# The first feed-forward product of a retention network, taken in two f32r parts in every step of the later layers

## Chip, cores and metric

The kernel runs on one core of one Trainium2 chip. The metric is the device time of one execution in microseconds (us); the figure given for a kernel is the median over several runs.

## What is computed

The input x holds 8 sequences of 512 tokens with 128 features. It is normalized, and two branches start from the result: four layers of a retention network (here "attn"), and one layer of eight experts of which each token uses one (here "ffn"). The reference, cut to what matters:

```python
def block(h, p):                                  # one of four layers
    wk, w1, b1, w2, b2, gg, gb, wf1, bf1_, wf2, bf2_, lg, lb = p
    r = _retention(h, wk)
    m = r @ w1 + b1
    a, gate = jnp.split(m, 2, axis=-1)
    m = a * jax.nn.silu(gate) @ w2 + b2
    m = _groupnorm1(m, gg, gb)
    y = m + h
    f = jax.nn.gelu(y @ wf1 + bf1_, approximate=False) @ wf2 + bf2_
    return (_layernorm(f + y, lg, lb), None)

# experts: each token through the one with the greatest router logit
h = jax.nn.gelu(x_flat @ w1[e] + b1[e], approximate=False)
y = h @ w2[e] + b2[e]
# result
xn = _layernorm(x, axis=-1)
g = _silu(_L0_ffn_ref(xn, gate_w, w1, b1, w2, b2))
x = x + s * g                                     # s: the four layers' output
```

The change is about `y @ wf1`: 128 features into 256, for 512 tokens of one sequence at a time.

## The kernel before

Work goes in steps `(l, t)`: layer l from 0 to 3, t from 0 to 7, and three steps behind them. A step is a slot of a software pipeline over the 32 pairs of layer and sequence. Step t takes sequence t through the retention, sequence t-1 through the gate and the second product up to `y_sb`, sequence t-2 through the feed-forward part (`gelu_first`, `gelu_second`), and sequence t-3 through its LayerNorm and back into both layouts, `htok` (tokens on the partitions) and `hT` (features on the partitions). Every engine has its own hand-written order of the step's pieces, and the engines meet by semaphores. Each engine works through its own list in order.

The experts' work is cut in 39 tiles of 128 slots, worked off in the steps of layers 1 to 3. A step has two places for a tile, EARLY and LATE. `TURNS` (L263) gives the steps t = 0, 3 and 5 only the LATE place and the other five both:

```python
TURNS = [[LATE] if t in (0, 3, 5) else [EARLY, LATE] for t in range(B)]
```

A tile's first product ends in `bank5`, and ScalarE takes it through four Gelus of 128x128 into `h_T` (`tile_gelu`, L612, instructions of L618). For the LATE tile of step t this is done at the end of the same step when step t+1 has an EARLY tile (L714), and otherwise within step t+1, as `tile_gelu(late_turn_before(l, t))` (L677). So the steps t = 0, 3 and 5 are those with four Gelus of the tile before in their midst.

The first feed-forward product is `gelu_first` (L1234), called twice in a step, for the halves k = 0 and k = 1 of the 256 output features; half k is written to `bank[3 + k]`. Bank 3 also holds the gate's product of the same step, which ScalarE reads twice, as `th_sb` (L629) and `gg_sb` (L631); the second reading raises `gg_done`. Half 0 waits for `gg_done` (L1247), half 1 does not.

The product has two forms. In the plain form it is one f32 product of `all_f1` and `y_sb` (L1255, two matrix instructions). In the parted form ScalarE rounds `y_sb` to f32r, `y_h` (L673), VectorE makes the rest, `y_l` = `y_sb` - `y_h` (L963), and `parts_product` (L1228) makes three f32r products into the same bank: L1230, L1231 and L1232. The weights' parts `f1_parts` are made once by GpSimd. `parted(l, t)` chooses the form, and with it three more things: the order of the halves (`halves`: 0, 1 if parted, otherwise 1, 0), the place of `zhat_by_feature` on TensorE (the transposes of the normalized rows, L1264, ahead of the halves if parted, otherwise behind), and the place of the gate's two readings on ScalarE:

```python
if not parted(l, t):
    gate(l, t)
layernorm(l, t)
tile_gelu(late_turn_before(l, t))
if parted(l, t):
    gate(l, t)
```

Names used below: `q_sb` is ScalarE's copy of the query product, `zhat` the LayerNorm's output (its first two quarters by VectorE, L1074, its last two by ScalarE, L640), `A_sb` the masked scores (VectorE, L971), L978 and L988 VectorE's two operations that join gate and value into `gg_sb`, L1372 the second product, L1359 and L1361 the retention's output.

Of the kernel before, what the change touches and what calls it, by code (L numbers as in the profile page):

```python
# [17 lines left out]
def retention_moe_kernel(nc, x, Wkqv, Wm1, bm1, Wm2, bm2, gn_g, gn_b, Wf1, bf1, Wf2, bf2, ln_g, ln_b,  # L18
# [9 lines left out]
    B, S, D = x.shape  # L28
    L = Wkqv.shape[0]
# [20 lines left out]
    with ctx:  # L50
# [210 lines left out]
        EARLY, LATE = range(2)  # L261
        FIRST_TURNS = [(B - 1, EARLY), (B - 1, LATE)]
        TURNS = [[LATE] if t in (0, 3, 5) else [EARLY, LATE] for t in range(B)]  # L263
        assert sum(map(len, TURNS)) == TURN_TILES and EARLY not in TURNS[0]

        def turn(l, t, place):


            if isinstance(l, int) and (l == 0 or l >= L):
                if l == 0 and (t, place) in FIRST_TURNS:  # L270
                    j = FIRST_TURNS.index((t, place))
                    return j, TURN_TILES - TILE_LAG + j
                return None
            if place not in TURNS[t]:
                return None
            k = sum(map(len, TURNS[:t])) + TURNS[t].index(place)
            return (l - 1) * TURN_TILES + TILE_LAG + k, k
# [10 lines left out]
        def parted(l, t):  # L288


            return turn(l, t, EARLY) is not None and not (l == 0)

        def parted_steps(l, t):

            early = [k for k in range(B) if EARLY in TURNS[k]]
            return (l - 1) * len(early) + early.index(t) + 1

        def halves(l, t):

            return (0, 1) if parted(l, t) else (1, 0)  # L300
# [291 lines left out]
        def _(act):  # L592
# [72 lines left out]
            def step(l, t):  # L665
# [4 lines left out]
                if parted(l, t):  # L670
                    w = at(l, t, 2, B, LB)
                    act.wait_ge(y_done, w[0] + 1)
                    act.activation(y_h[:, :], y_sb[:, :], ACT.Copy).then_inc(y_high, 1)  # L673
                if not parted(l, t):
                    gate(l, t)
# [45 lines left out]
        def _(dve):  # L721
# [227 lines left out]
            def step(l, t):  # L949
# [11 lines left out]
                if parted(l, t):  # L961
                    dve.wait_ge(y_high, parted_steps(l, t))
                    dve.tensor_tensor(y_l[:, :], y_sb[:, :], y_h[:, :], ALU.subtract).then_inc(y_split, 1)  # L963
# [155 lines left out]
        def _(pe):  # L1119
# [114 lines left out]
            def gelu_first(l, t, i):  # L1234

                if w := at(l, t, 2, B, LB):
                    n, b, li = w
                    k = halves(l, t)[i]
                    if parted(l, t):
                        if t in (1, 2):  # L1240
                            pe.wait_ge(part_made, parts_made("f1", li))
                        pe.wait_ge(y_split, parted_steps(l, t))
                    else:
                        pe.wait_ge(y_done, n + 1)
                    need(pe, G_done, 2 * n)
                    if k == 0:
                        need(pe, gg_done, n + 2 if not (isinstance(n, int) and n + 2 > LB) else LB)  # L1247
                    else:
                        if not (l == 0):
                            need(pe, xtT_done, turns_before(l, t, LATE))  # L1250
                    cols = slice(k * D, (k + 1) * D)
                    if parted(l, t):
                        parts_product(bank[3 + k], f1_parts[:, li], cols, y_h, y_l, pe_f1)
                    else:
                        mm(bank[3 + k][:, :], all_f1[:, li, cols], y_sb[:, :], start=True, stop=True).then_inc(pe_f1, 1)  # L1255
# [167 lines left out]
```

## Time and profile before

| | us |
|---|---|
| median of 3 runs | 517.68 |
| lowest and highest | 517.53, 518.33 |
| profiled execution, device time | 517.43 |
| profiled execution, span in the trace | 515.4 |
| TensorE busy in the span | 469.9 (91%) |
| VectorE busy | 386.7 (75%) |
| ScalarE busy | 261.5 (51%) |
| GpSimd busy | 251.6 (49%) |

Engines are named PE (TensorE matrix instructions), PEld (its weight loads), DVE (VectorE), ACT (ScalarE), POOL (GpSimd) and SP (SyncE) in the profile. Times in a row are microseconds from the span's start. The 2.0 us between the span and the device time lie around the span.

### The profile page before, as it was taken

The numbers are of one execution on the slowest core, as the hardware profiler recorded it, in microseconds if no ns is written. First come the engines' busy times: TensorE is split into PE (matmuls) and PEld (weight loads), VectorE is DVE, ScalarE is ACT, GpSimd is POOL, SyncE is SP. The second block draws the span as 40 slices with busy tenths as digits, with TensorE's granted clock in tenths as the row PEclk, the third lists the DMA queues.
The fourth block names the chain that finished last, engine by engine and source line by source line (L and its number), as shares of the span: only waits on it lengthen the run. The fifth ranks groups of instructions, "written<-read, shape, count | busy, mean of one in ns | idle before, by whom it ended". The sixth has DMA issues, their size and how long they took to land.

```text
span 515.4 us, 9900 instructions
## 1 busy us (share of the span) xinstructions
PE 469.9 (91%) x3179; PEld 393.7 (76%) x3179; DVE 386.7 (75%) x1342; ACT 261.5 (51%) x561; POOL 251.6 (49%) x304
## 2 busy tenths in 40 slices
PE   7999899999999999999999999999999999999400
PEld 5887666667888898888898888988889888886300
DVE  4768888878777777866777777787767777777896
ACT  3822434444566565454556565655555565665710
POOL 4570288887444443345444344434454443444663
PEclk9998999999999999999999999999999999999955
DMA  9999611113211011111011110111011010105014
GB/s 256 233 142 190 204 36 37 36 38 68 58 58 63 32 58 37 35 61 63 29 40 58 33 63 31 58 42 59 31 63 40 30 58 31 63 33 150 25 41 122
DMA packets 48833, 36.16 MB, mean 70 GB/s; under 512 B 13960, under 2 KB 39888, under 8 KB 48784
## 3 DMA queue, kind: packets, MB, share of 16 engines
q1 hardware_dynamic: 45824, 29.73, 22.5%
q0 software_dynamic: 2432, 5.02, 3.4%
q10 hardware_dynamic: 528, 0.79, 0.5%
q8 instruction: 27, 0.44, 0.4%
q14 instruction: 22, 0.18, 0.1%
HBM read 14.85 MB, written 9.84 MB: 48 GB/s over the span
## 4 chain that ended last, share of the span: by engine, by line
PE 71%; POOL 10%; DVE 8%; issue 5%; DMA 2%; ACT 1%; SPq 0%; DVEq 0%; POOLq 0%
PE bank L1290 9%; PE bank L1219 7%; PE bank L1199 7%; POOL x_slots L494 6%; PE pair L1335 5%; PE pair L1359 4%; PE pair L1317 4%; PE bank L1372 4%; PE bank L1230 4%; PE bank L1231 4%; PE bank L1232 4%; PE pair L1315 3%; PE pair L1361 3%; PE bank L1255 3%; PE bank L1288 2%
## 5 line engine op out<-in xcount | busy, mean ns | idle before, releaser
L517 POOL TENSOR_TENSOR zhat<-zhat,all_lg 128x512 f32<-128x512 f32 x31 | 40.6, 1309 | 96.0 <-PE bank L1264 95.7
L1290 PE MATMUL bank<-all_f,G_sb 128*128 128x128 f32 x512 | 72.9, 275 | 0.0
L712 ACT ACTIVATE y_sb<-bank,gn_bi,gn_sc 128x512 f32<-128x512 f32 x32 | 24.9, 778 | 94.3 <-DVE gn_bi L1055 94.3
L707 ACT ACTIVATE uT_h<-bank 128x512 fp32r<-128x512 f32 x32 | 19.1, 597 | 99.6 <-PE bank L1274 99.6
L564 POOL DMA_INDIRECT y_rows<-yt,tile_ids x39 | 40.3, 1033 | 58.1 <-DVE yt L1101 51.4
L1290 PEld LDWEIGHTS bank<-all_f,G_sb 128*128 128x128 f32 x512 | 67.4, 192 | 1.4 <-issue 1.4
L1199 PEld LDWEIGHTS bank<-moe_w,h_T 128*128 128x128 f32 x312 | 39.7, 191 | 14.6 <-issue 14.6
L450 POOL TENSOR_TENSOR ln_rs<-ln_ve,half_neg 128x4 f32<-128x4 f32 x32 | 33.1, 1035 | 29.4 <-DVE ln_ve L736 29.1
L618 ACT ACTIVATE h_T<-bank,w_t 128x128 f32<-128x128 f32 x156 | 44.6, 375 | 4.6 <-PE bank L1219 4.6
L1219 PE MATMUL bank<-xtT,w_t 128*128 128x128 f32 x320 | 44.6, 282 | 0.1
L689 ACT ACTIVATE G_sb<-bank,all_par 128x512 f32<-128x512 f32 x64 | 42.6, 703 | 1.7
L1000 DVE TENSOR_TENSOR rs<-pair,floor_sb 128x4 f32<-128x4 f32 x32 | 5.2, 161 | 50.0 <-PE pair L1361 50.0
L1199 PE MATMUL bank<-moe_w,h_T 128*128 x312 | 41.7, 277 | 0.0
L521 POOL TENSOR_TENSOR htok<-zhat,all_lb 128x512 f32<-128x512 f32 x31 | 39.7, 1282 | 2.4
L1219 PEld LDWEIGHTS bank<-xtT,w_t 128*128 128x128 f32 x320 | 38.9, 192 | 0.5 <-issue 0.5
L536 POOL TENSOR_TENSOR gn_rs<-gn_ve,half_neg 128x1 f32<-128x1 f32 x32 | 18.2, 569 | 41.1 <-DVE gn_ve L947 41.0
L1255 PE MATMUL bank<-y_sb,all_f 128*128 128x512 f32 x68 | 32.7, 603 | 5.4 <-DVE y_sb L1065 5.3
L1230 PE MATMUL bank<-uT_h,all_w 128*128 128x512 f32 x64 | 36.3, 566 | 1.2 <-DVE uT_l L935 1.1
L1361 PE MATMUL pair<-S_sb,q_sb 128*128 128x129 f32 x192 | 37.1, 275 | 0.0
L494 POOL DMA_INDIRECT x_slots<-xn,pos x32 | 32.4, 1011 | 8.0 <-issue 8.0
L1288 PE MATMUL bank<-ident,y_sb 128*128 128x128 f32 x128 | 35.0, 273 | 1.3 <-ACT hT L695 1.3
L640 ACT ACTIVATE zhat<-bank,ln_nb,ln_rs 128x128 f32<-128x128 f32 x64 | 26.3, 474 | 16.2 <-DVE zhat L1074 16.2
(181 smaller groups left out, 1243.3 us busy)
## 6 DMA issues: line engine op xcount, KB each, us to landing
w_t<-moe_w SPq DMA_DIRECT2D x41, 258.0 KB, 2.3
xt<-x_slots SPq DMA_DIRECT2D x41, 65.0 KB, 1.8
x_slots<-moe_w SPq DMA_DIRECT2D x1, 2644.5 KB
x_sb<-in_L_attn_x SPq DMA_DIRECT2D x8, 256.0 KB, 6.0
moe_w<-in_L_ffn_w SPq DMA_DIRECT2D x1, 2048.0 KB, 19.1
moe_w<-y_rows SPq DMA_DIRECT2D x8, 256.0 KB, 4.7
out<-moe_w SPq DMA_DIRECT2D x8, 256.0 KB, 2.2
all_f<-in_L_attn_Wf SPq DMA_DIRECT2D x2, 512.0 KB, 5.3
```

Of the source, the lines that this page charges most:

```text
L494: pool.indirect_dma_start(x_slots[:, :], bass.IndirectOffsetOnAxis(ap=pos[:, k:k + 1], axis=0), xn[:, k, :], None).then_inc(scattered, 16)
L517: pool.tensor_tensor(zhat[:, b % 2, :, :], zhat[:, b % 2, :, :], all_lg[:, li, :].unsqueeze(1).broadcast_to([P, C, D]), ALU.mult)\
L564: pool.indirect_dma_start(y_rows[:, :], bass.IndirectOffsetOnAxis(ap=tile_ids[q][:, :], axis=0), yt[q][:, :], None).then_inc(yt_out[q], 16)
L618: last = act.activation(h_T[:, i * P:(i + 1) * P], bank[5][:, i * P:(i + 1) * P], ACT.Gelu, bias=w1_t[buffer_of((k - 1) % TURN_TILES)][:, ...
L689: act.activation(G_sb[:, k, :], bank[3 + k][:, :], ACT.Gelu, bias=all_par[:, w[2], F_B + k:F_B + k + 1]).then_inc(G_done, 1)
L1199: last = mm(bank[5][:, 0:D], h_T[:, i * P:(i + 1) * P], moe_w2[:, bass.ds(e, 1), i, :].rearrange("p a d -> p (a d)"), start=i == 0, stop=i ...
L1219: last = mm(bank[5][:, i * P:(i + 1) * P], w1_t[q][:, i * P:(i + 1) * P], xtT[:, :], start=True, stop=True)
L1230: mm(dst[:, :], weights[:, 0, cols], high[:, :], start=True, stop=False)
L1255: mm(bank[3 + k][:, :], all_f1[:, li, cols], y_sb[:, :], start=True, stop=True).then_inc(pe_f1, 1)
L1288: mm(bank[7][:, at_c], y_sb[:, at_c], ident[:, :], start=True, stop=False, is_transpose=True)
L1290: last = mm(bank[7][:, at_c], G_sb[:, k, at_c], all_f2[:, li, k, :], start=False, stop=k == 1)
L1361: last = mm(dst, q_sb[:, c * P:(c + 1) * P], S_sb[:, c - 1, :], start=False, stop=True)
```

## The change

`parted` becomes true for every step of layers 1 to 3, so for t = 0, 3 and 5 as well. `parted_steps`, which counts the parted steps for the semaphore values, is changed to match.

```diff
         def parted(l, t):
 
 
-            return turn(l, t, EARLY) is not None and not (l == 0)
+            return 0 < l < L
 
         def parted_steps(l, t):
 
-            early = [k for k in range(B) if EARLY in TURNS[k]]
-            return (l - 1) * len(early) + early.index(t) + 1
+            return (l - 1) * B + t + 1
```

All that hangs on `parted` moves with it in the nine steps (three in each of three layers). The kernel after is one line shorter, so its line numbers are one less from here on: L629 of before is L628 of after.

The two instruction orders below are of layer 2, t = 0. First ScalarE. `th_sb` and `gg_sb` are the gate's readings of bank 3, `h_T` the four Gelus of the expert tile, `G_sb` the Gelus of the first product's halves. Before:

```order
L663 ACTIVATE q_sb<-pair 128x512 [waits pe_q]
L629 ACTIVATE th_sb<-bank3,all_par 128x512 [waits pe_g]
L631 ACTIVATE gg_sb<-bank3,all_par 128x512
L640 ACTIVATE zhat<-bank7,ln_nb,ln_rs 128x128 [waits z_half]
L640 ACTIVATE zhat<-bank7,ln_nb,ln_rs 128x128
L618 ACTIVATE h_T<-bank5,w1_t3 128x128 [waits pe_h]
L618 ACTIVATE h_T<-bank5,w1_t3 128x128 x3
L689 ACTIVATE G_sb<-bank4,all_par 128x512 [waits pe_f1]
L689 ACTIVATE G_sb<-bank3,all_par 128x512 [waits pe_f1]
```

And after:

```order
L662 ACTIVATE q_sb<-pair 128x512 [waits pe_q]
L672 ACTIVATE y_h<-y_sb 128x512 [waits y_done]
L639 ACTIVATE zhat<-bank7,ln_nb,ln_rs 128x128 [waits z_half]
L639 ACTIVATE zhat<-bank7,ln_nb,ln_rs 128x128
L617 ACTIVATE h_T<-bank5,w1_t3 128x128 [waits pe_h]
L617 ACTIVATE h_T<-bank5,w1_t3 128x128 x3
L628 ACTIVATE th_sb<-bank3,all_par 128x512 [waits pe_g]
L630 ACTIVATE gg_sb<-bank3,all_par 128x512
L688 ACTIVATE G_sb<-bank3,all_par 128x512 [waits pe_f1]
L688 ACTIVATE G_sb<-bank4,all_par 128x512 [waits pe_f1]
```

The rounding `y_h` has come in behind the queries, and the gate's two readings have moved from ahead of the LayerNorm to behind the four expert Gelus.

Then TensorE in the same step, from the scores' product on. Before:

```order
L1335 MATMUL pair<-q_sb,hT 128x128 x3
L1255 MATMUL bank4<-y_sb,all_f1 128x512 [waits xtT_done,G_done,y_done]
L1255 MATMUL bank3<-y_sb,all_f1 128x512 [waits gg_done,G_done,y_done]
L1264 MATMUL bank7<-ident,zhat 128x128 [waits z_done]
L1264 MATMUL bank7<-ident,zhat 128x128 x3
L1359 MATMUL pair<-htok,A_sb 128x129 [waits S_done,A_done]
```

And after:

```order
L1334 MATMUL pair<-q_sb,hT 128x128 x3
L1263 MATMUL bank7<-ident,zhat 128x128 [waits z_done]
L1263 MATMUL bank7<-ident,zhat 128x128 x3
L1229 MATMUL bank3<-y_h,f1_parts 128x512 [waits gg_done,G_done,y_split]
L1230 MATMUL bank3<-y_h,f1_parts 128x512
L1231 MATMUL bank3<-y_l,f1_parts 128x512
L1229 MATMUL bank4<-y_h,f1_parts 128x512 [waits xtT_done,G_done,y_split]
L1230 MATMUL bank4<-y_h,f1_parts 128x512
L1231 MATMUL bank4<-y_l,f1_parts 128x512
L1358 MATMUL pair<-htok,A_sb 128x129 [waits S_done,A_done]
```

Two f32 products have become six f32r ones, the transposes of `zhat` stand ahead of them, and bank 3, which waits for `gg_done`, is the first bank written instead of the second. On VectorE one operation comes in, `y_l` (L962 of after), between the last sum into `S_sb` (L957) and `A_sb` (L970).

## Rows read from the trace of the kernel before

**Rows 1.** Page: span, and busy time by engine.

```profile
span 515.4 us, 9900 instructions
PE 469.9 (91%) x3179; PEld 393.7 (76%) x3179; DVE 386.7 (75%) x1342; ACT 261.5 (51%) x561; POOL 251.6 (49%) x304
```

**Rows 2.** Windows, a stretch of layer 2: busy PE, PEld, DVE, ACT, POOL; clock; DMA.

```profile
243.00:283.00 40.00, 39.99 (x285) 34.80 (x284) 29.38 (x99) 23.26 (x52) 17.11 (x21) 1.00 0.14 48
```

**Rows 3.** Timeline of PE, layer 2, t = 0: start, length, instructions.

```profile
241.52 0.83 PE L1315 MATMUL pair<-htok 128*128 128x129 f32 x6
...
245.34 1.88 PE L1255 MATMUL bank<-y_sb,all_f 128*128 128x512 f32 x4
...
247.49 0.61 PE L1359 MATMUL pair<-htok,A_sb 128*128 128x129 f32 x4
...
249.06 1.02 PE L1372 MATMUL bank<-gg_sb,all_w 128*128 128x512 f32 x2
...
251.24 0.27 PE L1288 MATMUL bank<-ident,y_sb 128*128 128x128 f32 x1
```

**Rows 4.** Timeline of ACT in the same step; in brackets idle time before.

```profile
243.25 0.60 ACT L663 ACTIVATE q_sb<-pair 128x512 f32<-128x512 f32 x1
243.95 0.69 ACT L629 ACTIVATE th_sb<-bank,all_par 128x512 f32<-128x512 f32 x1
244.53 0.68 ACT L631 ACTIVATE gg_sb<-bank,all_par 128x512 f32<-128x512 f32 x1
245.10 0.81 ACT L640 ACTIVATE zhat<-bank,ln_nb,ln_rs 128x128 f32<-128x128 f32 x2
245.79 1.16 ACT L618 ACTIVATE h_T<-bank,w_t 128x128 f32<-128x128 f32 x4
246.79 1.31 ACT L689 ACTIVATE G_sb<-bank,all_par 128x512 f32<-128x512 f32 x2
...
251.44 0.60 ACT L707 ACTIVATE uT_h<-bank 128x512 fp32r<-128x512 f32 x1 [2.67 <-PE bank L1274]
```

**Rows 5.** Timeline of DVE in the same step.

```profile
243.24 0.69 DVE L1065 TENSOR_TENSOR y_sb<-y_sb,hT 128x512 f32<-128x512 f32 x1 [0.16 <-ACT y_sb L712]
...
244.28 0.73 DVE L1074 TENSOR_SCALAR zhat<-bank,ln_rs,ln_nb 128x128 f32<-128x128 f32 x2
...
245.78 0.68 DVE L971 TENSOR_TENSOR A_sb<-pair,causal 128x512 f32<-128x512 f32 x1
```

**Rows 6.** Timelines of ACT, DVE, PE in the next step, t = 1, already parted.

```profile
257.76 0.66 ACT L673 ACTIVATE y_h<-y_sb 128x512 fp32r<-128x512 f32 x1
...
259.73 0.69 ACT L631 ACTIVATE gg_sb<-bank,all_par 128x512 f32<-128x512 f32 x1
...
259.38 0.68 DVE L963 TENSOR_TENSOR y_l<-y_sb,y_h 128x512 fp32r<-128x512 f32 x1
...
260.69 0.60 PE L1264 MATMUL bank<-ident,zhat 128*128 128x128 f32 x4
261.04 0.48 PE L1230 MATMUL bank<-y_h,f_parts 128*128 128x512 f32 x1
```

**Rows 7.** Chain that ended last: start, share of the chain, what ran.

```profile
245.50 1.72 PE bank L1255 x4
...
261.29 0.23 PE bank L1230
...
262.69 0.45 PE pair L1359 x4
```

**Rows 8.** Timeline behind the last layer: a product that waited, and its releaser.

```profile
470.53 0.69 DVE L1065 TENSOR_TENSOR y_sb<-y_sb,hT 128x512 f32<-128x512 f32 x1 [0.16 <-ACT y_sb L712]
...
471.28 1.98 PE L1255 MATMUL bank<-y_sb,all_f 128*128 128x512 f32 x4 [0.90 <-DVE y_sb L1065]
```

**Rows 9.** Windows with little matrix work, columns as in Rows 2.

```profile
44.00:50.00 6.00, 6.00 (x28) 4.19 (x28) 4.07 (x18) 2.44 (x4) 0.58 (x1) 0.72 0.99 259
477.00:481.00 4.00, 0.59 (x7) 0.50 (x6) 2.83 (x16) 2.24 (x7) 1.56 (x2) 1.00 0.18 55
```

## The prediction

> **What bounds the kernel now.** I read the page's busy shares first, then the windows, then the chain, then the timelines of one step. TensorE is busy for 91% of the span [rows 1]. That is an average over stages, so the windows decide: in a stretch of 40 us inside layers 1 to 3 the engine is busy for 39.99 us, at a granted clock of 1.00, which is 2.4 GHz [rows 2]. No other engine is near that; ScalarE has 23 of 40 us and VectorE 29. In these layers every microsecond of TensorE is on the path, and the chain that ended last is TensorE piece after piece. Two things follow. A shorter product gives back its whole saving, as long as its inputs are there in time. And since nothing else covers it, any wait on TensorE is paid in full. So the question is not how much work ScalarE and VectorE gain, but when the values that TensorE waits for arrive in the new order.
>
> **The product itself.** In a step that changes, the chain has 1.72 us for the two plain halves (four records of L1255) [rows 7]. In a parted step it has six pieces of 0.23 us, from 261.29 to the 262.69 at which L1359 takes over, so 1.40 us [rows 7]. The saving is 0.32 us a step. There are nine changed steps (t = 0, 3, 5 in three layers), so 2.9 us in all if nothing waits. The transposes L1264 only change places and cost the same.
>
> The rate is where the Trainium skill differs from the row. Its page "TensorE: Matmul & The Clock Gate", section "Back-to-back issue gap", gives about 131 ns a matmul of 512 columns in a stream of weight loads and matmuls. This trace shows 233 ns, so the page's figure doesn't hold here for f32r. An estimate by that page: six of them would take 0.79 us instead of 1.40, the saving would be 0.93 us a step, and the time below would come out 5.5 us lower.
>
> **What moves on ScalarE.** I replay the step of layer 2, t = 0. It is preceded by a step that doesn't change, so everything that enters it arrives as in the trace. `q_sb` runs from 243.25 to 243.85 [rows 4]. `y_h` then needs `y_sb`, which VectorE ends at 243.24 + 0.69 = 243.93 [rows 5], so it starts at about 243.96. Its length is 0.66 us [rows 6]; consecutive activations of that width start 0.58 apart (243.95 and 244.53 [rows 4]), so the engine is free for the next at 244.55. The LayerNorm needs VectorE's half, ended at 244.28 + 0.73 = 245.01 [rows 5]. It starts at 245.04 and ends at 245.85, 0.81 later [rows 4]. The four expert Gelus follow 0.69 behind its start, as 245.10 and 245.79 do [rows 4], at 245.73. The instruction behind them starts 1.00 later (245.79 to 246.79 [rows 4]), so the gate's `th_sb` starts at 246.73 instead of 243.95, `gg_sb` at 247.31, and `gg_done` comes at 247.31 + 0.68 = 247.99. Before, it came at 245.21. That is the whole case: the gate's readings arrive 2.8 us later.
>
> **What TensorE meets.** Its scores' product ends where L1255 started, at 245.34 [rows 3]. The first thing there is now the transposes of `zhat`, which wait for the LayerNorm at 245.85. The hand-over from another engine to TensorE costs 0.06 us (VectorE ends at 470.53 + 0.69 = 471.22, L1255 starts at 471.28 [rows 8]). So they start at about 245.91, a stall of 0.57 us, and their four records are over by 246.51 (0.60 [rows 6]). The next is half 0 into bank 3, which waits for `gg_done`, so it starts at 247.99 + 0.06 = 248.05. TensorE stands for another 1.5 us. Then come the six parts. Started from idle, the first has its full length instead of overlapping the one before: 0.48 at most [rows 6]. With five more of 0.233 the last ends at 249.70. Records that follow closely start 0.16 before the end of the one before (L1255 is recorded at 245.34 [rows 3] and has its share of the chain from 245.50 [rows 7]), so L1359 would be recorded at 249.54, against 247.49 [rows 3]. The step is **2.05 us longer**. The lower bound of this term takes 0.39 for the first part and no hand-over, 1.9 us. For the upper one, a product that started from idle took 1.98 instead of 1.88 us [rows 3, 8], twice 0.1 for two restarts, and 0.1 more for a late hand-over on ScalarE: 2.35 us. I take 2.05, by the rows of this very step.
>
> **What else is added, and what covers it.** `y_l` on VectorE is 0.68 us [rows 6]. It stands ahead of `A_sb`, which moves from 245.78 to about 246.4 and ends at 247.1. TensorE asks for it at 249.5, so there are 2.4 us of cover; without the stall the cover would have been about 0.1 us. Behind it VectorE's two gate operations now wait for `gg_done` and end near 249.5 (247.99 plus 0.7 and 0.75). L1372 needs them, and it comes 1.57 behind L1359 (247.49 to 249.06 [rows 3]), so at 251.1; 1.6 us to spare. On ScalarE the Gelus of the halves come at about 249.1 and 249.8 and `hT` ends by 251.2. TensorE asks for all three at L1288, 251.24 + 2.05 = 253.3 [rows 3]. ScalarE had 2.67 us idle ahead of `uT_h` [rows 4], which takes the rest. GpSimd gets the transposes' release earlier relative to L1359, which helps nobody. SyncE's loads wait for an expert transpose later in the step and move with it. Nothing is late at the step's end, so the step after starts as before, only 2.05 us later, and the effect neither grows nor fades.
>
> **Sum.** 9 x 2.05 = 18.4 us. Against the profiled execution, 517.43 us, that is 535.9. That execution is 0.25 below the median of the runs shown, so the forecast for the median is **536.1 us**, 3.6% slower. With the term's bounds, 17.1 and 21.2 us, it is 534.8 to 538.8.
>
> **Rivals.** *The product's saving arrives in full.* Then the nine steps lose 0.32 us each and the time is 514.8, faster. For it speaks that the 15 parted steps run with no idle time on TensorE. But there `gg_sb` ends at 259.73 + 0.69 = 260.42, ahead of the first part at 261.04 [rows 6], because the tile before had its Gelus at the end of the step before, and an expert product on TensorE gives ScalarE time. Neither holds for t = 0, 3 and 5. It decides at 246.35, where TensorE is through with the transposes: `gg_done` would have to come 1.6 us earlier than worked out.
>
> *Only the LayerNorm's wait is paid.* If the gate were in time and the transposes of `zhat` alone stalled for 0.57 us, a step would cost 0.57 - 0.32 + 0.1 for the restart, about 0.35 us, and the time would be 520.8. It needs ScalarE to run the expert Gelus in a fifth of their 1.00 us; no row shows that.
>
> *The clock falls in the stalls.* TensorE has 2.5 us in each changed step with four transposes and nothing else. In the window 44 to 50 us, behind a run of products of a single column, the granted clock averaged 0.72 with the engine recorded as busy throughout; that is 6.00 x 0.28 = 1.7 us lost in one fall to 1.2 GHz. Against it, in the window 477 to 481 us TensorE was busy for only 0.59 us of 4 and the clock stayed at 1.00 [rows 9]. Once in each of nine steps it would add 9 x 1.7 = 15 us and give 551; in some of them, something between. The same page of the Trainium skill, section "HAM oscillation — how this bites in real kernels", warns that waits between groups of matmuls can put the engine to half its clock again and again. [...]
>
> **Chances.** Forecast, 534.8 to 538.8: 0.84. Saving in full, 514.8: 0.04. LayerNorm only, 520.8: 0.03. Clock falls, 540 to 551: 0.09. The range is 533.8 to 540.0: the forecast's bounds, widened by 1 us for what the replay rounds off, and it leaves the rivals outside. Against no change within 0.2%, about what a measurement of this kernel can tell: faster 0.04, same 0.02, slower 0.94.
>
> **What would show it.** In the trace of after, each of the nine steps should have ScalarE's order `q_sb`, `y_h`, `zhat`, `h_T`, `th_sb`, `gg_sb` without a gap from 2.5 us behind the step's first TensorE instruction on; an idle time of about 0.4 us ahead of L1263, released by `zhat`; one of about 1.5 us ahead of the first L1229 with `y_h`, released by `gg_sb`; six parts 0.23 apart; and L1358 at 8.0 us into the step instead of 6.0. TensorE's idle time should grow by some 17 us in total. The windows of layers 1 to 3 should show a clock of 1.00. The 15 other steps should be as long as they were. I would be wrong if ScalarE's waits let `gg_sb` end before 247.5 on the scale of before, if a later wait in the step (L1372, L1288) comes up as a new stall, or if the clock leaves 1.00.

## The result, and the profile after

| | before | after |
|---|---|---|
| median, us | 517.61 (4 runs) | 540.56 (4 runs) |
| lowest and highest, us | 517.43, 518.33 | 538.24, 541.53 |
| span of the profiled execution, us | 515.4 | 539.8 |

The change makes the kernel slower, by a factor of 1.0437 with a 95% interval of 1.0413 to 1.0461. The direction and the waits were forecast. The falls of the clock were not in the forecast, nor was the size: 22.9 us against 18.4, and 540.56 lies just above the range that ended at 540.0. A second thing changed that the table shows: the kernel before repeats within 0.9 us, the kernel after spreads over 3.3.

The head of the page of after, which answers [rows 1]:

```profile
span 539.8 us, 9954 instructions
PE 477.0 (88%) x3197; PEld 403.4 (75%) x3197; DVE 400.7 (74%) x1351; ACT 269.3 (50%) x570; POOL 255.9 (47%) x304
```

TensorE is busy for 7.1 us more, in a span that is 24.4 us longer. 4.8 of the 7.1 are three steps in which its clock fell (14.8 to 14.9 us busy instead of 13.3, windows below). Who it waited for is in the list of TensorE's waits (us in total, times, longest one), of which the upper lines are:

```profile
PE bank L1229 <- ACT gg_sb L630: 14.6, 9, 1.6
PE bank L1254 <- DVE y_sb L1064: 6.0, 8, 3.4
PE bank L1263 <- ACT zhat L639: 5.1, 12, 0.7
```

The first is new, with nine instances, one for each changed step: the first part waits for the gate's second reading. Of the third's twelve instances, nine are in the changed steps: the transposes wait for the LayerNorm. The second is of layer 0 and of the steps behind the last layer, and was there before.

One changed step (layer 2, t = 0) on the timelines of PE and ACT, to be read against [rows 3] and [rows 4], which are 8.27 us earlier:

```profile
249.79 0.83 PE L1314 MATMUL pair<-htok 128*128 128x129 f32 x6
...
254.19 0.66 PE L1263 MATMUL bank<-ident,zhat 128*128 128x128 f32 x4 [0.41 <-ACT zhat L639]
256.47 0.47 PE L1229 MATMUL bank<-y_h,f_parts 128*128 128x512 f32 x1 [1.63 <-ACT gg_sb L630]
...
257.95 0.61 PE L1358 MATMUL pair<-htok,A_sb 128*128 128x129 f32 x4
...
265.14 0.83 PE L1314 MATMUL pair<-htok 128*128 128x129 f32 x6
```

```profile
252.24 0.63 ACT L672 ACTIVATE y_h<-y_sb 128x512 fp32r<-128x512 f32 x1
253.33 0.81 ACT L639 ACTIVATE zhat<-bank,ln_nb,ln_rs 128x128 f32<-128x128 f32 x2 [0.45 <-DVE zhat L1073]
254.03 1.14 ACT L617 ACTIVATE h_T<-bank,w_t 128x128 f32<-128x128 f32 x4
...
255.03 0.72 ACT L628 ACTIVATE th_sb<-bank,all_par 128x512 f32<-128x512 f32 x1
255.60 0.73 ACT L630 ACTIVATE gg_sb<-bank,all_par 128x512 f32<-128x512 f32 x1
```

The step is 15.35 us long, from 249.79 to 265.14. The kernel before took 13.17 for it, so it is 2.18 us longer. Six of the nine steps have this length. The other three are those where the clock fell. Windows of two changed steps, one of each kind (columns as in [rows 2]: length, busy PE, PEld, DVE, ACT, POOL, then the granted clock):

```profile
324.93:340.28 15.35, 13.30 (x93) 11.41 (x92) 11.69 (x38) 7.65 (x15) 5.78 (x7) 1.00 0.08 27
414.86:431.83 16.97, 14.93 (x94) 12.90 (x92) 11.70 (x38) 7.65 (x15) 5.78 (x7) 0.90 0.07 25
```

The timeline of PE inside the second shows how:

```profile
421.54 0.47 PE L1229 MATMUL bank<-y_h,f_parts 128*128 128x512 f32 x1 [1.63 <-ACT gg_sb L630]
421.85 0.40 PE L1230 MATMUL bank<-y_h,f_parts 128*128 128x512 f32 x1
422.09 0.39 PE L1231 MATMUL bank<-y_l,f_parts 128*128 128x512 f32 x1
422.32 0.47 PE L1229 MATMUL bank<-y_h,f_parts 128*128 128x512 f32 x1
422.58 0.63 PE L1230 MATMUL bank<-y_h,f_parts 128*128 128x512 f32 x1
423.01 0.63 PE L1231 MATMUL bank<-y_l,f_parts 128*128 128x512 f32 x1
```

The first four parts start 0.23 to 0.31 us apart at 2.4 GHz. Then the clock goes to 1.2 GHz, and the last two start 0.43 apart; it is back at 2.4 GHz at about 426. The stretch before the fall had the two idle times and four transposes, and no product. The three steps are 17.18, 16.97 and 16.88 us long. The first of them, in layer 1, has a longer wait for the LayerNorm besides (0.64 instead of 0.41 us); the kernel with dummy products below takes 15.56 us for it without a fall. So the falls cost 1.62, 1.62 and 1.53 us.

**The account.** Nine steps longer by 2.18 us are 19.6, the longer wait in the first is 0.2, three falls are 4.8. In the kernel before, two unchanged steps, t = 1 of layers 1 and 2, were 15.16 and 15.03 us long; after, both are 14.82: 0.6 back. In them TensorE's expert product (L1219) came late behind VectorE's `yt` (L1101), which it waits for. In layer 1 of the kernel before:

```profile
145.40 0.29 DVE L1101 TENSOR_TENSOR yt<-bank,moe_b 128x128 f32<-128x128 f32 x1 [0.25 <-issue]
145.84 1.13 PE L1219 MATMUL bank<-xtT,w_t 128*128 128x128 f32 x8
```

I took these two for waits on loads that longer steps hide, and the expectations below say so. The runs contradict it: with the gate late in the kernel before, the changed steps are 2 us longer and the two are still there (15.16 and 15.05), and the refitted kernel, whose steps are shorter, doesn't have them. Every kernel that takes the parted product in the nine steps is without them. Why is open. The stretch ahead of the first changed step and the one behind the last are 0.3 longer together. That makes 24.3 of the 24.4 us by which the span grew.

### The profile page after: what moved, and what is told of

Its sections match the earlier page's. It is cut to its first block, busy times and chain, and to the rows that moved or that the text cites. A ratio compares the mean times of both kernels' runs of the same rounds, so it can differ in the third digit from the quotient of the medians.

```text
span 539.8 us, 9954 instructions
## 1 busy us (share of the span) xinstructions
PE 477.0 (88%) x3197; PEld 403.4 (75%) x3197; DVE 400.7 (74%) x1351; ACT 269.3 (50%) x570; POOL 255.9 (47%) x304
## 4 chain that ended last, share of the span: by engine, by line
PE 60%; DVE 14%; POOL 10%; ACT 7%; issue 6%; DMA 2%; SPq 0%; DVEq 0%; POOLq 0%
PE bank L1289 9%; PE bank L1198 7%; PE bank L1218 5%; PE pair L1358 5%; POOL x_slots L493 5%; PE bank L1229 4%; PE bank L1371 4%; PE bank L1230 4%; PE bank L1231 4%; PE pair L1360 3%; POOL ln_rs L449 3%; PE pair L1334 3%; PE pair L1316 3%; PE bank L1287 2%; PE bank L1273 2%
## 5 line engine op out<-in xcount | busy, mean ns | idle before, releaser
L1289 PE MATMUL bank<-all_f,G_sb 128*128 128x128 f32 x512 | 74.6, 279 | 0.0
L1289 PEld LDWEIGHTS bank<-all_f,G_sb 128*128 128x128 f32 x512 | 69.0, 196 | 1.4 <-issue 1.4
L1360 PE MATMUL pair<-S_sb,q_sb 128*128 128x129 f32 x192 | 38.2, 281 | 0.0
L977 DVE SCALAR_TENSOR_TENSOR gg_sb<-th_sb,gg_sb 128x512 f32<-128x512 f32 x32 | 30.3, 948 | 9.1 <-ACT gg_sb L630 9.1
L1287 PE MATMUL bank<-ident,y_sb 128*128 128x128 f32 x128 | 35.6, 278 | 1.0 <-ACT hT L694 1.0
```

The source lines that it names most:

```text
L1287: mm(bank[7][:, at_c], y_sb[:, at_c], ident[:, :], start=True, stop=False, is_transpose=True)
L1289: last = mm(bank[7][:, at_c], G_sb[:, k, at_c], all_f2[:, li, k, :], start=False, stop=k == 1)
L1360: last = mm(dst, q_sb[:, c * P:(c + 1) * P], S_sb[:, c - 1, :], start=False, stop=True)
```

## The experiments

All are built on the kernel before or after and were measured beside runs of the kernel before on the same chip (median 517.52 in both groups).

### Idle time filled with dummy products

```diff
                 if parted(l, t):
                     zhat_by_feature(l, t)
+                if parted(l, t) and EARLY not in TURNS[t]:
+                    pe.wait_ge(y_done, at(l, t, 2, B, LB)[0] + 1)
+                    keep_warm(3)
                 gelu_first(l, t, 0)
```

> The changed kernel with three dummy f32 products (128x256, into bank 6, free there) put on TensorE between the transposes of zhat and the first part, in the nine steps alone. Theory: the two stalls stay as they are for the step's length (they are ScalarE's), so the nine steps keep 15.35 us; but the falls of the granted clock, which cost three of them 1.5 to 1.8 us each, come from TensorE having only four transposes in 2.5 us, and go. Median 517.6 + 9 x 2.18 = 537.2, less up to 0.6 for two waits on loads that the longer steps hide, so 536.6 to 537.2, and all runs within 0.5 us of each other, where the changed kernel's ran from 538.2 to 541.5. Rival, the falls have nothing to do with the stalls (they would then come from the f32r products themselves or from power): one to three nine-step falls stay, runs spread from 538 to 542, median near 540.6.

Measured: 536.49 us (536.38 to 537.26, 5 runs), ratio 1.0364 (1.0350 to 1.0378). The same step of the timeline of PE:

```profile
253.35 0.66 PE L1263 MATMUL bank<-ident,zhat 128*128 128x128 f32 x4 [0.42 <-ACT zhat L639]
253.84 1.46 PE L1150 MATMUL bank<-ones,ident 128*128 128x256 f32 x6
255.63 0.47 PE L1229 MATMUL bank<-y_h,f_parts 128*128 128x512 f32 x1 [0.32 <-ACT gg_sb L630]
```

And the window over all three layers, of this kernel, then of the changed one:

```profile
127.00:480.00 353.00, 346.14 (x2442) 303.31 (x2441) 262.48 (x906) 191.69 (x412) 146.22 (x170) 1.00 0.14 46
```

```profile
127.00:480.00 353.00, 334.39 (x2349) 293.65 (x2349) 258.73 (x895) 188.13 (x403) 145.34 (x170) 0.99 0.14 44
```

TensorE does more here, 54 matrix instructions that nobody reads, and the kernel is 4.1 us faster than the changed one. The nine steps are 15.33 to 15.35 us, apart from the first with 15.56. No fall is left in the three layers. Four of the five runs lie within 0.12 us; the fifth, the profiled one, is 0.8 us longer, and its clock was at half for a stretch near 12 us, far ahead of the layers (window 12.4 to 15.6: 0.50). The length of the steps is therefore ScalarE's, and the falls come from TensorE standing without products. The rival, that f32r products or power bring the clock down, is out: the same products ran here at 1.00.

### The gate ahead of the expert Gelus

```diff
                 layernorm(l, t)
-                tile_gelu(late_turn_before(l, t))
                 if parted(l, t):
                     gate(l, t)
+                tile_gelu(late_turn_before(l, t))
```

> The changed kernel with ScalarE's gate readings ahead of the four expert Gelus, but still behind the LayerNorm, in the nine steps. Theory: gg_done comes exactly the four Gelus, 1.00 us, earlier; the idle time ahead of the first part falls from 1.63 to 0.63, the one ahead of the transposes stays 0.42; each of the nine steps is 1.18 us longer than in the kernel before, no clock falls: 517.6 + 10.6 = 528.2, with the two hidden load waits 527.6 to 528.3. Rival, that the added y_h and y_l and not the gate's place make the step long: step stays near 15.35, time stays above 536.

Measured: 527.08 us (526.94 to 528.23, 4 runs), ratio 1.0189 (1.0174 to 1.0205). TensorE's waits:

```profile
PE bank L1229 <- ACT gg_sb L630: 5.3, 9, 0.6
PE bank L1263 <- ACT zhat L639: 5.2, 13, 0.7
```

The wait for the gate falls from 1.63 to 0.59 us in each step, by the 1.0 us that the four Gelus take. The wait for the LayerNorm stays. The steps are 14.31 us, 1.14 longer than before, where I had 1.18; over nine steps that is 0.4 us, and the time is 0.5 below my 527.6 to 528.3. No fall shows in the window of the layers.

### The gate first, as before the change

```diff
-                if not parted(l, t):
+                early = parted(l, t) and EARLY in TURNS[t]
+                if not early:
                     gate(l, t)
                 layernorm(l, t)
                 tile_gelu(late_turn_before(l, t))
-                if parted(l, t):
+                if early:
                     gate(l, t)
```

> The changed kernel with ScalarE's gate readings where they were before the change, ahead of the LayerNorm, in the nine steps; TensorE's order is still the changed one. Theory: gg_done is in time (y_h costs it 0.6 us, no more), the idle time ahead of the first part goes to nothing; but the LayerNorm ends 0.66 us later, so the transposes of zhat wait about 1.07 us by the record instead of 0.42. Each of the nine steps 0.98 to 1.1 us longer than in the kernel before: 517.6 + 9 = 526.4 to 527.5, no clock falls. Rival, the gate's place is all there is to it: no stall left and the saving of 0.32 us a step comes in full, 514.8.

Measured: 524.73 us (524.65 to 524.81, 4 runs), ratio 1.0138 (1.0123 to 1.0154). The top of TensorE's waits:

```profile
PE bank L1264 <- ACT zhat L639: 10.4, 13, 1.1
```

The gate is gone from the list. The transposes now wait 1.00 us in each step instead of 0.42, since the LayerNorm stands behind the gate. The steps are 14.08 us, 0.9 longer than before. My 526.4 to 527.5 is at least 1.7 us too high, since I had counted 0.98 to 1.1 a step and left out the 0.6 us of the two t = 1 steps. What holds against the rival is the order of the result: with the gate in its old place the change still loses 1.4%, because it has moved `zhat_by_feature` too.

### The gate late, in the kernel before

The plain product, and only the gate's place changed:

```diff
-                if not parted(l, t):
+                if not 0 < l < L:
                     gate(l, t)
                 layernorm(l, t)
                 tile_gelu(late_turn_before(l, t))
-                if parted(l, t):
+                if 0 < l < L:
                     gate(l, t)
```

> The kernel before with one part of the change alone: in the nine steps the gate's two readings stand behind the LayerNorm and the expert Gelus on ScalarE. The product stays the plain f32 one, half 1 first, and no y_h or y_l is made. Theory: gg_done comes at 6.6 us into the step as in the changed kernel (y_h had stood in a wait for the LayerNorm there and cost nothing); half 1 runs at 3.8 as before, and half 0 waits 1.8 us in one piece; each of the nine steps 1.8 to 2.0 us longer, 533.8 to 535.6. A single stall of 1.8 us behind full products lets no clock fall. Rival, that the gate's place costs only in company with the parted product: within 1 us of 517.6.

Measured: 536.49 us (536.26 to 537.96, 4 runs), ratio 1.0376 (1.0359 to 1.0392). The step of layer 2, t = 0 on PE:

```profile
251.80 1.02 PE L1255 MATMUL bank<-y_sb,all_f 128*128 128x512 f32 x2
254.65 1.10 PE L1255 MATMUL bank<-y_sb,all_f 128*128 128x512 f32 x2 [1.83 <-ACT gg_sb L631]
```

Half 1 runs, half 0 waits 1.83 us for `gg_sb`. The steps are 15.24 us, 2.07 longer than before. So one part of the change, with no f32r product in these steps, loses as much as the whole change without its falls (536.49 us both). I had 533.8 to 535.6, 0.9 us short. I had taken the idle time alone, 1.8 to 2.0. But the records of back-to-back instructions overlap by about 0.16 us and a product after idle takes 0.08 longer (1.10 against 1.02); both come on top. In its profile the clock stays at 1.00 over the three layers, with a single stall in each changed step (1.83 us, 2.05 in the first) and full products on both sides. One of its four runs, 537.96, is 1.4 us above the next; it has no profile, so a fall in it isn't excluded.

### Everything else put back, and the low part waited for where it is used

```diff
         def halves(l, t):
-            return (0, 1) if parted(l, t) else (1, 0)
+            return (0, 1) if parted(l, t) and EARLY in TURNS[t] else (1, 0)
...
                 mm(dst[:, :], weights[:, 1, cols], high[:, :], start=False, stop=False)
+                if low_made is not None:
+                    pe.wait_ge(y_split, low_made)
                 mm(dst[:, :], weights[:, 0, cols], low[:, :], start=False, stop=True).then_inc(done, 1)
...
-                        pe.wait_ge(y_split, parted_steps(l, t))
+                        pe.wait_ge(y_high, parted_steps(l, t))
```

The gate is first, as above, the transposes of `zhat` are behind the halves in the nine steps, and VectorE makes `y_l` there ahead of `S_sb`.

> All steps of layers 1 to 3 parted, as in the changed kernel, but in the nine steps everything else is as it was before the change: the gate's readings ahead of the LayerNorm, half 1 ahead of half 0, the transposes of zhat behind the halves. Besides, VectorE makes y_l ahead of its work on S_sb, and TensorE waits for y_h alone ahead of the first two parts and for y_l ahead of the third, in every parted step. Theory: y_h is there at 3.1 us into the step, y_l at 4.1, gg_sb at 4.4, zhat at 5.05; TensorE asks for them at 3.8, 4.3, 4.5 and 5.2, so it doesn't wait and the nine steps are 0.3 us shorter: 517.6 - 2.9 = 514.8, at worst 516.5 if one hand-over of 0.15 us shows in each. Rival, that f32r parts aren't cheaper than the f32 product where both are fed in time: 517.6 or more.

Measured: 514.60 us (514.33 to 515.23, 5 runs), ratio 0.9940 (0.9926 to 0.9953). Faster than both kernels. The step of layer 2, t = 0 on PE, then ACT's gate and DVE's `y_l`:

```profile
245.23 0.48 PE L1235 MATMUL bank<-y_h,f_parts 128*128 128x512 f32 x1
...
246.02 0.40 PE L1235 MATMUL bank<-y_h,f_parts 128*128 128x512 f32 x1
...
246.71 0.60 PE L1271 MATMUL bank<-ident,zhat 128*128 128x128 f32 x4
247.15 0.67 PE L1367 MATMUL pair<-htok,A_sb 128*128 128x129 f32 x4
```

```profile
245.04 0.68 ACT L630 ACTIVATE gg_sb<-bank,all_par 128x512 f32<-128x512 f32 x1
...
244.91 0.68 DVE L954 TENSOR_TENSOR y_l<-y_sb,y_h 128x512 fp32r<-128x512 f32 x1
```

No wait on the first product, the transposes or L1367 shows in these steps. They take 12.91 us, 0.26 less than before (the first of layer 1 takes 13.13, 0.05 less). `gg_sb` ends at 245.72 and bank 3's first part starts at 246.02. So the saving that the change is meant for is there. It shows only when the inputs come in time. It is 2.1 us in the nine steps, not 2.9; another 0.6 comes from the two t = 1 steps, which are 14.80 us here. The 15 steps that were parted already now wait for `y_l` at the third part too, and with those two apart they are as long as before. That 514.60 meets the expected 514.8 so well is in part luck.

### The same with `y_l` where the change puts it

VectorE makes `y_l` behind `S_sb` in the nine steps; the rest is as in the last kernel.

> The refitted kernel, but with y_l on VectorE where the change puts it, behind the work on S_sb. Theory: it is ready at 5.0 us into the step instead of 4.1, TensorE comes to the third part at 4.3 and stands for 0.65 to 0.75 us, so the nine steps are 13.5 to 13.7 us instead of 12.91 and the time is 520 to 521.5. That would show that y_l, which the changed kernel's own stalls cover, is the next thing late once they are gone. Rival, that the two parts of y_h and the load of weights cover it: 514.6 to 516.

Measured: 521.33 us (521.24 to 521.38, 4 runs), ratio 1.0073 (1.0057 to 1.0090). TensorE's waits have a new line:

```profile
PE bank L1237 <- DVE y_l L954: 5.2, 9, 0.8
```

In the step of layer 2, t = 0:

```profile
247.90 0.50 PE L1237 MATMUL bank<-y_l,f_parts 128*128 128x512 f32 x1 [0.56 <-DVE y_l L954]
```

The third part waits 0.56 us, and the steps are 13.67 us, 0.76 longer than with `y_l` early. Again the idle time by the record is less than the loss. In the changed kernel this wait is invisible, since the gate comes later still.

### The changed kernel once more

> The changed kernel once more, on the same chip as the two others. Theory: without falls of the clock in the nine steps it would take 536.5, as the kernel with the filled stalls; each fall adds about 1.6 us. So the single runs lie on steps at about 536.5, 538.1, 539.7, 541.3 and so on, and spread over more than 2 us. Rival, that the chip or the first measurement made the spread: all within 0.5 us.

Measured: 540.26 us (541.08, 537.90, 537.84, 541.03, 540.26), ratio 1.0420 (1.0392 to 1.0447). The spread is 3.2 us, so the kernel's own. Its profiled execution has the falls in the same three steps (17.18, 16.95 and 16.90 us long). The single runs don't lie on clean steps: 540.26 is between two of them. That much of the expectation didn't hold: the falls differ in length (1.5 to 1.6 us), and the kernel without them has runs 0.9 us apart as well.

## Why the prediction was right and wrong

**What bounds the kernel** was right. TensorE's waits and its clock are nearly the whole account; the two t = 1 steps are 0.6 us of it.

**ScalarE's replay** was right to 0.1 us. Moved by the 8.27 us between the two time scales, it had `th_sb` at 255.00 and `gg_sb` at 255.58; measured are 255.03 and 255.60. It had the transposes at 254.18, and they started at 254.19. Moving and restoring the gate's readings confirm it: the wait for the gate is 1.63 us with four Gelus ahead of it, 0.59 without them, and none in the old place.

**The term of 2.05 us a step** measured 2.18. The first part started at 256.47 where I had 256.32. About 0.07 of that is `gg_sb`, which started 0.02 later and took 0.73 us instead of 0.68. The other 0.08 is the hand-over to TensorE: 0.14 us, where I took 0.06 from [rows 8]. There VectorE hands over, but the pair of engines isn't the reason: in this very step the transposes start 0.05 us behind ScalarE's `zhat`. What makes the difference is open. Over nine steps the term was 1.2 us short.

**What covers the rest** was right for the changed kernel: L1371 and L1287 didn't wait. I had asked whether `A_sb`, behind `y_l`, would be in time without the stall, but not whether `y_l` itself would be. The run with `y_l` late in the refitted kernel shows it 0.56 us late. One row I had wrong: VectorE's gate operation took 1.75 us instead of 0.68 (last section), since the transposes' earlier release of GpSimd, of which I wrote only that it helps nobody, puts GpSimd's work beside it. The 1.6 us of slack ahead of L1371 took that.

**The clock** is the step that failed. The sum has nothing for it, and in its place the runs show 4.1 us (540.56 against 536.49 with the idle time filled). I had it as a rival only, gave that 0.09, priced it as a fall in each of the nine steps, 15 us, with 540 to 551 as its times, and left it outside the range. The words "in some of them, something between" were there, and the measured 540.56 lies at that rival's lower end, but nothing was worked out for them. I had two windows of [rows 9] that disagreed and read that as a rare event. What happens is in between: the stall with four transposes in it brings the clock down in some of the steps, three of nine in the profiled execution. The cost of one fall, 1.7 us from [rows 9], was nearly right (1.5 to 1.6). It should have been a term of the sum, 9 steps x a share between 0 and 1 x 1.7 us, and the range should have reached to it from below. With the filled idle time the kernel takes 536.49 us, which is 0.4 from the forecast of 536.1: that is the case I forecast. That it is so near is in part luck: 1.2 us missing in the term and 0.2 in the first step stand against 0.6 that the two t = 1 steps gave back. The falls are the 4.1 us on top, and they are why the time left the range.

The Trainium skill (page "TensorE: Matmul & The Clock Gate", section "HAM oscillation — how this bites in real kernels") describes waits between groups of matmuls that put the engine to half clock in each round of a loop. The runs agree in kind: the falls come in a third of the changed steps, and behind waits that are shorter than those of the page's example (0.41 and 1.63 us here). The figure of the same page's section "Back-to-back issue gap", 131 ns for a matmul of 512 columns in a stream, isn't borne out for these f32r products: at 2.4 GHz they follow each other about 233 ns apart in every kernel here.

**The rival of the full saving** needed `gg_done` at 246.35 on the time scale of before. The refitted kernel shows that this was not quite the condition. The gate had to be in time, and the transposes had to stand where the LayerNorm doesn't hold them, and `y_l` had to be early. With all three it gives 514.6, and the rival's price was 514.8; 0.6 us of that agreement comes from the two t = 1 steps and not from the product.

## What to carry to other kernels

A flag that picks a cheaper form may also pick an order; on an engine that is busy all the time, list what each moved piece waits for before counting the saving. Here 0.3 us of saving a step stood against about 2.5 us of waiting, and moving the pieces back turned 4% slower into 0.6% faster. Where a sum leaves the matrix engine without products for a stretch in which no run has shown that the clock holds (2.7 us here), add the clock as a term with a share of the cases, not as an all-or-nothing rival. And an idle time in the record understates its cost by 0.2 us or so, since overlap at the restart is lost too.

## What the runs showed of the hardware

VectorE's first gate operation, both inputs in SBUF (the memory next to the engines), took 1.73 to 1.76 us in eight of the nine steps, and 0.68 or 0.69 in the first of layer 1 and in all others. The timelines of POOL and DVE at that place of the changed kernel:

```profile
254.93 1.26 POOL L516 TENSOR_TENSOR zhat<-zhat,all_lg 128x512 f32<-128x512 f32 x1 [2.67 <-PE bank L1263]
256.27 1.29 POOL L520 TENSOR_TENSOR htok<-zhat,all_lb 128x512 f32<-128x512 f32 x1
...
256.36 1.75 DVE L977 SCALAR_TENSOR_TENSOR gg_sb<-th_sb,gg_sb 128x512 f32<-128x512 f32 x1 [1.01 <-ACT gg_sb L630]
```

GpSimd starts 0.09 us earlier and ends at 257.56. VectorE's operation ends at 258.11, about its own length later. So it stood for the whole of GpSimd's instruction. In the kernel with the gate ahead of the Gelus it took 1.44 us there, again in company of GpSimd. The Trainium skill, page "SBUF — State Buffer", section "SBUF: two separate sides", has this as an exclusive lock on the port pair that the two engines share, held for a whole instruction; the trace agrees, with 1.07 us of blocking. VectorE's second gate operation (L988 of before), which has one of its inputs in a bank, took 0.75 us in every run, also beside GpSimd. It takes both moves to bring the two together: with the gate late and the transposes where they were the operation took 0.69 us, with the transposes early and the gate first 0.68. No list of one engine shows such an effect.

The other one is the clock. A stall of 1.83 us in one piece between full products (2.05 in the first step) left it at 1.00 in the profiled execution. Idle times of 0.41 and 1.63 us with four transposes between them, 2.7 us without a product, brought it to half in three steps of nine, the same three in two profiled executions. With 0.41 and 0.59 us around the same transposes, 1.65 us without a product (the gate ahead of the Gelus), it stayed at 1.00. Dummy products in the longer idle time stopped the falls. So the transposes with short stalls don't do it. Whether the longer stretch alone does, or the transposes in it count as well, was not tried, and why only three of the nine steps fall is open.
